# Four graph-attention layers on one core: the order of the work between layers, and idle matmuls

## The reference

```python
h = jnp.maximum(_layernorm(x, axis=-1), 0.0)
x = x + _L0_gnn_ref(h, adj, ...)     # 8 heads, ELU, then @ W_out + b_out
x = x + _L1_gnn_ref(...)             # h again first; 1 head, exact GELU
x = x + _L2_gnn_ref(...)             # 1 head, ELU
x = x + _L3_gnn_ref(...)             # 1 head, ELU
# inside each layer, for each head:
Wh = h @ W;  s1 = Wh @ a1;  s2 = Wh @ a2
e = s1[:, None] + s2[None, :]; e = where(e > 0, e, 0.2 * e); e = where(adj > 0, e, -big)
out = nonlinear(softmax(e, axis=1) @ Wh)
```

## Time and profile before

| what | value |
|---|---|
| profiled execution | 763.28 us |
| its span, first to last instruction | 761.6 us |
| outside the span | 1.7 us |
| TensorE matmul busy | 744.0 us (98%) |
| TensorE weight load busy | 729.2 us (96%) |
| VectorE busy | 619.9 us (81%) |
| ScalarE busy | 325.9 us (43%) |
| mean granted TensorE clock | 0.996 |
| hole 1: last matmul of unit (0, 2) to first of unit (1, 0) | about 544.5 to 557.7 us |
| hole 2 | about 619.3 to 629.0 us |
| hole 3 | about 689.6 to 699.3 us |

### The profile page before, as it was taken

How to read it: one execution, slowest core, us unless ns; L and a number is a source line. 1 busy time by engine, 2 the same in 40 slices (tenths; PEclk the granted TensorE clock), 3 DMA queues, 4 the chain that set the end, 5 groups by cost and what they waited for, 6 DMA issues and landing times.

```text
span 761.6 us, 15996 instructions
## 1 busy us (share of the span) xinstructions
PE 744.0 (98%) x6467; PEld 729.2 (96%) x6467; DVE 619.9 (81%) x1048; ACT 325.9 (43%) x878; POOL 16.6 (2%) x38
## 2 busy tenths in 40 slices
PE   8999999999999999999999999999889989999997
PEld 8789999999999999999999999999789979997997
DVE  4988779797797967979788797878687959897986
ACT  4978341452443435144254324633440352636230
POOL 3000000000000000000000000000000000000000
PEclk9999999999999999999999999999999999999999
DMA  9993000000000000000000000000000000000001
GB/s 297 342 368 103 29 29 1 28 0 28 28 0 28 0 28 22 6 28 0 28 23 5 28 0 28 0 0 1 2 1 2 1 1 1 2 1 1 1 25 33
DMA packets 13874, 29.39 MB, mean 39 GB/s; under 512 B 1296, under 2 KB 7568, under 8 KB 13840
## 3 DMA queue, kind: packets, MB, share of 16 engines
q1 hardware_dynamic: 11152, 20.00, 7.7%
q0 software_dynamic: 2688, 8.92, 3.3%
HBM read 27.80 MB, written 1.11 MB: 38 GB/s over the span
## 4 chain that ended last, share of the span: by engine, by line
PE 94%; DVE 3%; ACT 1%; DMA 1%; issue 0%; DVEq 0%; ACTq 0%
PE acc L447 56%; PE acc L472 26%; PE side L571 3%; PE side L395 3%; PE acc L524 1%; PE side L511 1%; DMA X<-in_x_dram 1%; PE side L383 0%; DVE stats L1084 0%; PE side L497 0%; DVE probs L1267 0%; PE side L426 0%; PE acc L535 0%; PE side L367 0%; ACT adjT L693 0%
## 5 line engine op out<-in xcount | busy, mean ns | idle before, releaser
L447 PE MATMUL acc<-V,probs 128*128 128x129 f32 x3840 | 436.6, 275 | 1.5 <-DVE probs L1174 1.5
L447 PEld LDWEIGHTS acc<-V,probs 128*128 128x128 f32 x3840 | 432.6, 192 | 4.5 <-DVE V L1128 2.3
L1177 DVE SCALAR_TENSOR_TENSOR probs<-rho,t_now,adjT 128x1024 f32<-128x1024 f32 x238 | 290.0, 1277 | 13.9 <-PE acc L447 9.1
L1267 DVE SCALAR_TENSOR_TENSOR probs<-rho,t_now,adjT 128x768 f32<-128x768 f32 (+3 forms) x182 | 147.2, 868 | 14.8 <-PE acc L472 12.1
L790 ACT ACTIVATE hpT<-rows 32x256 f32<-32x256 f32 x224 | 92.8, 414 | 66.6 <-DVE rows L1214 64.2
L472 PE MATMUL acc<-stage,probs 128*128 128x129 f32 x1024 | 117.5, 277 | 2.4 <-DVE probs L1267 2.4
L472 PEld LDWEIGHTS acc<-stage,probs 128*128 128x128 f32 x1024 | 116.6, 194 | 2.8 <-issue 2.8
L472 PE MATMUL acc<-V,probs 128*128 128x129 f32 x768 | 89.4, 275 | 1.6 <-DVE probs L1267 1.6
L472 PEld LDWEIGHTS acc<-V,probs 128*128 128x128 f32 x768 | 87.4, 192 | 1.8 <-issue 1.8
L775 ACT ACTIVATE fill<-mean_now,empty 128x128 f32<-128x128 f32 x120 | 36.7, 395 | 89.8 <-DVE den L1190 89.8
L1222 DVE TENSOR_TENSOR X<-X,side 128x512 f32<-128x512 f32 x28 | 19.3, 688 | 65.9 <-PE side L571 65.9
(11 more groups left out here) (207 smaller groups left out, 395.8 us busy)
## 6 DMA issues: line engine op xcount, KB each, us to landing
stage<-in_adj_t_dram SPq DMA_DIRECT2D x24, 512.0 KB, 7.0
rho<-rho_dram POOLq DMA_DIRECT2D x15, 512.0 KB, 3.8
hpT<-in_adj_t_dram SPq DMA_DIRECT2D x4, 512.0 KB, 7.7
xn<-in_adj_t_dram SPq DMA_DIRECT2D x4, 512.0 KB, 6.5
X<-in_x_dram SPq DMA_DIRECT2D x2, 512.0 KB, 4.5
W0t<-in_W_t_dram SPq DMA_DIRECT2D x1, 512.0 KB, 5.2
W<-in_L_gnn_W_heads_dram SPq DMA_DIRECT2D x1, 512.0 KB, 6.5
Wout<-in_L_gnn_W_out_dram POOLq DMA_DIRECT2D x1, 512.0 KB, 9.7
```

The costliest lines, as they stand in the source:

```text
L447: last = nc.tensor.matmul(group(c, k), probs[:, j % RING, k * P:(k + 1) * P], V[:, j, :], start=(j == 0 and k % PER_BANK == 0), stop=(j == ...
L1177: nc.vector.scalar_tensor_tensor(probs[:, j % RING, :], rho[:, c * CH:(c + 1) * CH], t_now[:, j:j + 1], adjT[:, j, c * CH:(c + 1) * CH], A ...
L1267: return nc.vector.scalar_tensor_tensor(slot_of(n, p, j)[:, first:end], rho[:, at + first:at + end], t_now[:, j:j + 1], adjT[:, j, at + fi ...
```

## The change

- Unit (0, 2): the transposes of rows chunk (1, 1) and the two output products of chunks (1, 0) and (1, 1) come half a tile to a tile earlier.
- Hole 1, DVE: the division of the two last tiles is ahead of `late_scale(1, 1)`, and their ELU ahead of `late_norm(1, 1)`. ACT: `keep_wh(1)` is behind the exponentials, `keep_s1(1, 0)` and the last tiles' exponential are ahead of the normalizing, `late_copy_rows(2, 0)` is between its two parts, `late_relu(1, 2, 0)` ahead of `keep_s1(1, 1)`. PE: 8 idle matmuls after the two s1 products (they wait for `keep_s1(1, 0)`, whose PSUM place they write), then the last tiles' row transposes ahead of the `xn` transposes, and their product between these.
- All three holes, PE: the last tiles' `xn` transposes before (n = 2, 3) or right after (n = 1) the second `late_wh` of chunk 1; `late_s1(n, 2)` behind `spread_late_max`. Hole 2 had it ahead of the maximum (and so had hole 1, where it moves too); hole 3 had it behind already, and there the first half of `late_s1(3, 1)` moves between the two `xn` transposes of chunk 1.
- Hole 2, ACT: the table load behind `late_relu(2, 2, 0)`. Hole 3, ACT: `late_relu(3, 1, 1)` ahead of `late_inverse_root(3, 2)`, `late_relu(3, 2, 0)` ahead of `keep_s1(3, 0)`.
- All three holes: 4 idle matmuls at the end, behind `late_s1(n, 3)` and a wait for `keep_s1(n, 1)`.
- `vy_two`, a product of two columns, moves behind the third tile of unit (n, 0) on DVE.

```diff
@@ -31,7 +31,7 @@
     STAGE, SLOTS = 5, 7
     OUT_AT, DEN_AT = (10, 11), 7
     Q = 32
-    WARM_START = (20, 2)
+    WARM_START, WARM_ROWS, WARM_HOLE = (20, 2), 8, 4
     SMALLEST = 2.0 ** -126
     LOG_EXP = "natural_log_exp_and_others"
     MW = D + H
@@ -632,29 +632,35 @@
                 late_s1(n, 0, wh_kept, n)
                 if n == 1:
                     late_s1(n, 1, wh_kept, n)
+                    pe.wait_ge(s1_kept, 1)
+                    keep_warm(WARM_ROWS, acc[:, 0, 0, 0:P])
+                    transpose_rows(2, 0, wh_kept, 1)
                     transpose_normed(1, 1, 0, x_written, chunk_no(1, 1, 0))
+                    project_rows(2, 0)
                     transpose_normed(1, 1, 1, x_written, chunk_no(1, 1, 1))
-                    transpose_rows(2, 0, wh_kept, 1)
-                    project_rows(2, 0)
+                elif n == 2:
+                    transpose_normed(n, 1, 0, hT_ready, chunk_no(n, 0, 0))
+                    transpose_normed(n, 1, 1, hT_ready, chunk_no(n, 0, 1))
+                    late_s1(n, 1, wh_kept, n)
                 else:
                     transpose_normed(n, 1, 0, hT_ready, chunk_no(n, 0, 0))
+                    late_s1(n, 1, wh_kept, n, 0)
                     transpose_normed(n, 1, 1, hT_ready, chunk_no(n, 0, 1))
-                if n == 2:
-                    late_s1(n, 1, wh_kept, n)
                 late_wh(n, 1, 0)
-                late_wh(n, 1, 1)
-                if n < 3:
-                    late_s1(n, 2, hT_ready, chunk_no(n, 1, 0))
-                transpose_normed(n, 2, 0, x_written, chunk_no(n, 2, 0))
-                if n == 3:
-                    late_s1(n, 1, wh_kept, n, 0)
+                if n == 1:
+                    late_wh(n, 1, 1)
+                    transpose_normed(n, 2, 0, x_written, chunk_no(n, 2, 0))
+                else:
+                    transpose_normed(n, 2, 0, x_written, chunk_no(n, 2, 0))
+                    late_wh(n, 1, 1)
                 late_wh(n, 2, 0)
                 if n == 3:
                     late_s1(n, 1, wh_kept, n, 1)
                 spread_late_max(n)
-                if n == 3:
-                    late_s1(n, 2, hT_ready, chunk_no(n, 1, 0))
+                late_s1(n, 2, hT_ready, chunk_no(n, 1, 0))
                 late_s1(n, 3, hT_ready, chunk_no(n, 1, 1))
+                pe.wait_ge(s1_kept, 2 * n)
+                keep_warm(WARM_HOLE, acc[:, 0, 1, 0:P])
 
             late_unit(0, 1, {(0, 1): later_vectors,
                              (4, 1): lambda: transpose_rows(0, 0, waL_ready, 1),
@@ -665,9 +671,9 @@
                              (14, 1): lambda: transpose_normed(1, 0, 1, x_written, chunk_no(1, 0, 1)),
                              **scores_of_half(1, 15)})
             late_unit(0, 2, {(7, 0): lambda: transpose_rows(1, 0, hT_ready, 1),
-                             (8, 1): lambda: transpose_rows(1, 1, hT_ready, 2),
-                             (10, 0): lambda: project_rows(1, 0),
-                             (11, 0): lambda: project_rows(1, 1)})
+                             (8, 0): lambda: transpose_rows(1, 1, hT_ready, 2),
+                             (9, 0): lambda: project_rows(1, 0),
+                             (10, 1): lambda: project_rows(1, 1)})
             for n in range(1, 4):
                 rest_of_scores(n)
                 late_unit(n, 0, {} if n == 1 else
@@ -1015,22 +1021,22 @@
                 late_relu(n, 0, 0)
                 late_relu(n, 0, 1)
                 if n == 1:
-                    keep_wh(1)
                     late_exp_rows(1, 1, 0)
                     late_exp_rows(1, 1, 1)
+                    keep_wh(1)
                     late_copy_rows(1, 0)
                     late_copy_rows(1, 1)
                     late_inverse_root(1, 1)
+                    keep_s1(1, 0)
+                    late_exp_rows(1, 2, 0)
                     late_normed(1, 1, (0,))
-                    late_exp_rows(1, 2, 0)
+                    late_copy_rows(2, 0)
                     late_normed(1, 1, (1,))
-                    keep_s1(1, 0)
-                    late_copy_rows(2, 0)
                     late_relu(1, 1, 0)
                     late_relu(1, 1, 1)
                     late_inverse_root(1, 2)
+                    late_relu(1, 2, 0)
                     keep_s1(1, 1)
-                    late_relu(1, 2, 0)
                 elif n == 2:
                     nonlinear_late(2, 1)
                     keep_wh(2)
@@ -1040,8 +1046,8 @@
                     late_relu(2, 1, 1)
                     keep_s1(2, 0)
                     keep_s1(2, 1)
+                    late_relu(2, 2, 0)
                     nc.scalar.preload_act_table_set(LOG_EXP)
-                    late_relu(2, 2, 0)
                 else:
                     keep_wh(3)
                     late_exp_rows(3, 1, 0)
@@ -1051,10 +1057,10 @@
                     late_exp_rows(3, 2, 0)
                     late_normed(3, 1, (1,))
                     late_relu(3, 1, 0)
+                    late_relu(3, 1, 1)
                     late_inverse_root(3, 2)
-                    late_relu(3, 1, 1)
+                    late_relu(3, 2, 0)
                     keep_s1(3, 0)
-                    late_relu(3, 2, 0)
                     keep_s1(3, 1)
                 late_factors(n)
                 if n == 1:
@@ -1454,7 +1460,6 @@
                 dve.wait_ge(late_vexp_ready, n)
                 v0 = V_of[n % 2][:, 0, :]
                 nc.vector.tensor_scalar(v0[:, 0:D], v0[:, 0:D], v0[:, D:D + 1], None, ALU.mult).then_inc(late_v0_ready, 1)
-                nc.vector.tensor_tensor(vy_two[:, :], V_of[n % 2][:, TWO:NT, D], nwt[:, 0, TWO:NT], ALU.mult).then_inc(vy_ready, 1)
 
             def mean_elu(n):
 
@@ -1490,11 +1495,11 @@
             add_to_x(1, 1, 0)
             add_to_x(1, 1, 1)
             late_statistics(1, 1)
-            late_scale(1, 1)
             late_denominators(1, 2)
             late_divide(1, 2, 0)
+            late_scale(1, 1)
+            late_elu_rows(2, 0)
             late_norm(1, 1)
-            late_elu_rows(2, 0)
             add_to_x(1, 2, 0)
             late_statistics(1, 2)
             late_norm(1, 2)
@@ -1503,7 +1508,9 @@
                 take_scores(n, 1)
                 take_scores(n, 2)
                 late_center(n)
-                tiles(n, 0, 0, 12)
+                tiles(n, 0, 0, 3)
+                nc.vector.tensor_tensor(vy_two[:, :], V_of[n % 2][:, TWO:NT, D], nwt[:, 0, TWO:NT], ALU.mult).then_inc(vy_ready, 1)
+                tiles(n, 0, 3, 12)
                 if n > 1:
                     mean(n, n)
                 tiles(n, 0, 12, 16)
```

## The result

The changed kernel takes 758.67 us (median of 4 executions, 758.29 to 759.12) against 763.1 us (762.66 to 764.51) of the kernel before: ratio 0.9937, 95% interval 0.9918 to 0.9955. Forecast was 758.4, range 757.6 to 760.7. The size is right; one of the reasons given for it is not, as the experiments show.

The account below looks back on a forecast made before the run. TensorE's pace bounds the units (94% of the waits), and the rest is in the three holes. 763.28 - 1.52 - 1.19 - 0.96 - 0.98 + 0.3 = 758.93, less 0.49 for the median gives 758.4 us, range 757.6 to 760.7.

Parts of the forecast that it names:

- Term 1: Tiles behind hole 1: idle matmuls keep TensorE's clock from falling to 0.50, gaining 1.52 us.
- With both filled: Hole 1: idle matmuls fill TensorE's idle 1.38 us mid-hole and 1.64 us at the end, so the clock stays up.
- about 1.2 us, ahead of the maximum: Hole 1: the longest TensorE idle time left after the change, shorter than hole 2's 1.7 us without a fall.
- Term 2: Hole 1's new order: the last two tiles' score comes at 553.08 instead of 554.27, gaining 1.19 us.
- Term 3: Hole 2: last transposes and relu come earlier, DVE's Newton steps bind next, table load hidden; gain 0.96 us.
- Term 4: Hole 3: relu and the last transposes come earlier, score at 694.81; gain 0.98 us.
- Term 5: End of each hole: 2.95 us of TensorE work in 3.01 us; 0.1 us late per hole, 0.3 lost in all.
- A: Rival: the clock still falls once, in this hole or another; 759.9 us, chance 0.15.
- B: Rival: two of the three holes' orders give nothing, as ACT or DVE is late next; 760.5 us, chance 0.12.
- D: Rival: gained time comes back in the units, by DVE; chance 0.04.
- C: Rival: idle matmuls exposed, hole 1's fully and the end ones by 0.3 us more each; 760.5 us, chance 0.07.
- E: Rival: slower, clock falls inside holes ahead of the maximum, +2.9 us per hole; 765.5 us, chance 0.03.

Follow-up runs that it names:

- no_idle: Changed kernel without any of its 20 idle matmuls in the holes, orders kept; 758.04 us, ratio 0.9932.
- before_end_idle: Kernel before plus only 4 idle matmuls and the wait for the copy of s1 at each hole's end; 761.46 us, ratio 0.9979.
- s1_behind: Kernel before with one edit, late_s1(n, 2) behind the spread of the maximum in holes 1 and 2 too; 761.31 us, ratio 0.9981.
- no_idle_newton2: Changed kernel without idle matmuls, and two instead of three Newton steps for the two last tiles in hole 2; 757.75 us, ratio 0.9932.
- table_first: Changed kernel without idle matmuls, and hole 2's table load ahead of late_relu(2, 2, 0) as in the kernel before; 758.63 us, ratio 0.9944.
- end8: Changed kernel with 8 instead of 4 idle matmuls at each hole's end; 761.17 us, ratio 0.9969.
- no_end_idle: Changed kernel without the 4 idle matmuls at each hole's end, the 8 in the middle of hole 1 kept; 758.54 us, ratio 0.9939.
- holes23_only: Kernel before with the new orders of holes 2 and 3 alone, no idle matmuls; 760.74 us, ratio 0.9962.

## Why the prediction was right, and where it was not

- **What bounds, and the yardstick.** Right: the last link stayed 3.01 us, and each hole is shorter by as much as the score comes earlier.
- **Term 1, the clock: 1.52 predicted, 1.63 in the trace, but for the wrong reason.** The step that failed is "With both filled", with the whole 1.52 us put down to the idle matmuls: no_idle has none of them and no fall either. The orders do it, among other things by moving `late_s1(n, 2)` into the idle time ahead of the unit, which is 0.79 us in no_idle instead of 1.64. That idle time matters, as the step says, is borne out by before_end_idle and s1_behind. The idle time "about 1.2 us, ahead of the maximum" was wrong too: it is 0.58 us in hole 1 of the changed kernel (the row of L559 above). Nor is it one fall per execution: the kernel before runs from 761.20 to 766.09 us at mean clocks of 1.000 to 0.993, and 42 of its 49 executions lie 1.2 us or more above the fastest; the median of the 49 is 2.0 us above it, that of the nine of the changed kernel 0.2 above its own 758.29. The profiled execution happened to have one fall at a hole and so to lie near the typical one; that 1.52 fitted is luck. Compared at their fastest, without falls, the kernels differ by 761.2 - 758.3 = 2.9 us, the orders' 2.8.
- **Term 2, hole 1: 1.19 predicted, 1.00 measured.** The idle matmuls were to cost 0.6, and cost 0.69. The other 0.1 is handovers: counted from s1's start, the row transposes came at 3.60 instead of 3.54, the last transposes (551.77) at 7.09 instead of 6.94, and the score at 8.80 instead of 8.62.
- **Term 3, hole 2: 0.96 predicted, 0.97 measured.** Its account of the next bound (DVE's Newton steps, TensorE 0.3 behind) and of the table load is shown by no_idle_newton2 and table_first.
- **Term 4, hole 3: 0.98 predicted, 0.82 measured.** The mis-sized part is the way to the last product: the score follows the s1 start by 5.38 us (691.59 - 686.21) instead of the 5.23 worked out. Its transposes start 0.1 us later than one handover behind `late_wh`, and relu (690.33) 0.05 more.
- **Term 5: 0.3 predicted, 0 measured.** The issue sum was exact (2.95 of 3.01; end8), and the wait for a long finished copy costs nothing: without both (no_end_idle) the holes are no shorter. The allowance was needless.
- **Sum.** Terms 2, 4 and 5 missed by 0.19, 0.16 and -0.3, which nearly cancel; that the sum is as close as 758.4 against 758.67 is therefore in part luck, while terms 2 to 4 were right in their mechanism.
- **Rivals.** A (one fall stays) didn't happen in nine executions of the changed kernel. B: all three orders gave what they were to give within 0.2 us. D: nothing came back in the units (47.59 us behind hole 2, 47.58 before). C: the 0.69 in hole 1 is the only idle work that was exposed. E (a fall inside a hole, slower) exists as a mechanism in other orders, but at half of what I gave it or less: 1.56 us in hole 1 of before_end_idle, 0.73 in the last link of s1_behind, not 2.9.

## What to carry to other kernels

Where an engine waits in a serial stretch, move needed work into the idle time before filling it with idle work: here the orders shortened the holes and the low clocks all but went with them, while the 8 idle matmuls stood in front of work that was ready. Idle matmuls are worth a try where no needed work can be moved: 4 of them ahead of each unit took 1.9 us off the median of the kernel before. What one execution shows once (one fall, 1.5 us) is a sample: look at the spread of many before it becomes a term of a sum. The version to keep here is the orders without idle matmuls (758.04 and 758.38 us in two sets, against 758.67 and 758.45), or with two Newton steps for the last tiles (757.75; 0.34 us less in hole 2), if that accuracy is enough.

## What the runs showed of the hardware that was not expected

- The granted clock fell to 0.50 for about three microseconds at a time, and not at the same places in each execution of a program: near 12 us in 6 of 14 profiles (before, after and end8 among them), near 22 in holes23_only, at 549 in before_end_idle and s1_behind, at 558 in the kernel before and holes23_only, at 624 in s1_behind. The Trainium skill's statement that the observation runs freely ("TensorE: Matmul & The Clock Gate", Part 1) fits that executions of one program differ; it doesn't say how often a fall comes, and in these runs that hangs on the program (42 of 49 executions before, 0 of 9 changed).
- At 0.50 only TensorE's work gets longer: in the middle of hole 1 of before_end_idle 12 instructions of `late_wh` take 2.88 us instead of 1.61, while DVE's addition keeps its 0.42 us and ACT's copy of s1 its 0.58. What a fall costs depends on what it meets: 1.5 to 1.6 us in the tiles behind a hole, 1.56 in the middle of hole 1, 0.73 in the last link of hole 2 (s1_behind).
